# Second pass over grouped count blocks, third pass with one exponent per slot, in a graph kernel on one Trainium2 core

## What is computed

```python
def sage(x, W_l, b_l, W_r):                 # first layer pair, called twice (32 -> 64, relu, 64 -> 32)
    agg = segment_sum(x[src], dst)
    return agg @ W_l.T + b_l + x @ W_r.T
x = layernorm(x + sage(relu(sage(x, ...)), ...))
en, ev = (x @ W2s + b2s)[src], (x @ W2d + b2d)[dst]          # 2 heads x 32
e = sum(leaky_relu(en + ev) * attn, -1)                      # one score for each edge and head
alpha = segment_softmax(e, dst)
msg = softmax(en * r * alpha, axis=-1)                       # over the 32 features of a head
x = layernorm(x + (x + segment_sum(msg, dst).sum(heads)) @ W1 + b1)
```

## Time and profile before

| | us |
|---|---|
| runs, median of 3 (lowest to highest) | 4073.04 (4067.71 to 4081.34) |
| the profiled execution's own time | 4068.59 |
| its span, first to last instruction | 4066.6 |
| first pass and set-up, until the gathers of the second begin | 1091.7 |
| second pass, first gather to the stage after it | 1091.7 to 1801.5 |
| third pass, first gather to the end of the last | 1870.0 to 3898.5 |
| messages of the last slots, output | 3898.5 to 4066.6 |

### The profile page before, as it was taken

One profiled execution on the slowest core, in us unless ns is written; L12 is line 12 of the kernel. 1 busy time (PEld: TensorE's weight loads), 2 busy tenths in 40 slices (PEclk: granted clock), 3 DMA queues, 4 the chain that ended last, 5 costly groups with the idle time before them and its releaser, 6 DMA issues. The chain is left out here.

```text
span 4066.6 us, 79597 instructions
## 1 busy us (share of the span) xinstructions
PE 3054.0 (75%) x26497; PEld 2336.8 (57%) x26497; DVE 2564.1 (63%) x7531; ACT 2697.1 (66%) x7419; POOL 2903.5 (71%) x2913
## 2 busy tenths in 40 slices
PE   4899999999798998885566666766766667666655
PEld 2555555666466666665465555665656666556544
DVE  7987766555422222235357777778777787777776
ACT  4888888778665556641056767777668766677745
POOL 4677777776377777755777777777777777777735
PEclk9999999999899999997657777777667776677767
DMA  2455565555588888853333333333333433343311
GB/s 79 186 207 207 211 234 208 206 207 206 195 310 279 291 289 284 284 173 107 64 86 85 83 81 87 89 86 84 79 82 93 91 83 83 77 92 87 87 31 41
DMA packets 294489, 592.92 MB, mean 146 GB/s; under 512 B 121210, under 2 KB 205364, under 8 KB 286169
## 3 DMA queue, kind: packets, MB, share of 16 engines
q1 hardware_dynamic: 203920, 515.15, 36.0%
q0 software_dynamic: 88192, 72.56, 11.0%
q10 hardware_dynamic: 1969, 0.10, 0.0%
HBM read 384.60 MB, written 202.94 MB: 144 GB/s over the span
## 5 line engine op out<-in xcount | busy, mean ns | idle before, releaser
L897 ACT ACTIVATE scratch<-sum_x_ps_c 128x600 bf16<-128x600 f32 (+7 forms) x1003 | 775.4, 826 | 168.1 <-PE sum_x_ps_c L934 156.5
L1945 POOL DMA_INDIRECT scratch<-fs_scratch,src_idx x728 | 725.3, 996 | 221.9 <-issue 221.9
L834 POOL DMA_INDIRECT gath<-in_x,src_idx x620 | 673.2, 1086 | 277.4 <-issue 182.4
L834 POOL DMA_INDIRECT gath<-y_scratch,src_idx x540 | 524.2, 971 | 171.6 <-issue 163.4
L2073 ACT ACTIVATE scratch<-scratch,bias,weight 128x32 f32<-128x32 f32 x1360 | 484.0, 399 | 101.5 <-DVE bias L2143 101.5
L1987 PEld LDWEIGHTS ps_e<-fdw,scratch 128*128 128x128 f32 x3136 | 500.4, 242 | 24.2
L934 PE MATMUL sum_x_ps_c<-e_tab,scratch 128*128 128x300 bf16 (+7 forms) x2006 | 472.9, 323 | 51.9 <-DVE scratch L1012 32.3
L1009 DVE TENSOR_SCALAR e_tab<-scratch 128x1300 bf16<-128x1300 f16 (+13 forms) x1024 | 455.7, 458 | 61.0 <-PE sum_x_ps_c L934 53.0
L1987 PE MATMUL ps_e<-fdw,scratch 128*128 128x66 f32 x3136 | 482.7, 322 | 0.0
L2154 DVE SCALAR_TENSOR_TENSOR scratch<-ps_e,attn_sb 128x128 f32<-128x128 f32 x784 | 190.2, 285 | 424.3 <-PE ps_e L1987 423.3
L963 PEld LDWEIGHTS sum_x_ps_d<-parts,scratch 128*128 128x128 bf16 x5800 | 337.1, 98 | 158.7 <-ACT scratch L897 68.0
(11 more groups left out here) (341 smaller groups left out, 6362.9 us busy)
## 6 DMA issues: line engine op xcount, KB each, us to landing
count_scratch<-scratch SPq DMA_DIRECT2D x58, 3200.0 KB
scratch<-count_scratch SPq DMA_DIRECT2D x232, 800.0 KB
onehot<-rel_scratch SPq DMA_DIRECT2D x196, 256.0 KB
scratch<-in_edge_attr_2x SPq DMA_DIRECT2D x390, 128.0 KB
fdw<-fd_scratch SPq DMA_DIRECT2D x392, 33.0 KB
scratch<-fs_scratch,src_idx POOLq DMA_INDIRECT x728
gath<-in_x,src_idx POOLq DMA_INDIRECT x652
gath<-y_scratch,src_idx POOLq DMA_INDIRECT x540
```

Source lines behind the costliest of these rows:

```text
L834: pool.indirect_dma_start(out=gath[:, s, t, 0:F], out_offset=None, in_=table_dram, in_offset=bass.IndirectOffsetOnAxis(ap=src_idx[:, g, k: ...
L897: act.activation(to, ps_c[u % pairs][:, :, 0:q].rearrange("p h (d a) -> p h a d", d=d), ACT.Copy).then_inc(kept, 1)
L1945: pool.indirect_dma_start(out=rows_of(m)[:, t, :], out_offset=None, in_=fs_dram, in_offset=bass.IndirectOffsetOnAxis(ap=src_idx[:, g, k:k ...
```

## The change

In the second pass the 58 read blocks are taken in groups of 4 (the last has 2). The roles of the operands are swapped: the 96 feature columns of one high index are the weights, and the counts of 4 blocks (4 x 128 columns) move, so that a group takes 100 matmuls of 512 columns into a 96 x 512 result. It is loaded in 10 pieces of 10 high indices, 4 pieces in flight in four buffers (two of them in memory that the features leave free, so the fourth waits for the cut of the features). After a group ACT copies the result (copy), PE turns it back and adds the three parts with 4 small matmuls (turn), DVE builds 4 placements and copies (spread), PE moves 4 windows, DVE adds them. The steps of the plan are now pieces.

In the third pass, for slots with a step m, DVE subtracts the maxima from the rows and multiplies with the attention weights (two tensor_tensor of 128 x 512 with broadcast operands), ACT runs one exponent of 128 x 512, and DVE sums all of it (L2178 becomes 128 x 512). The copy and the biases go. The one-hots of even slots move from DVE to ACT.

```diff
-QUARTERS = 4
-SHARES = 2 * QUARTERS
+TOGETHER = 4
+HIGHS = 10
+PIECES = ALL_HIGHS // HIGHS
+HELD_PIECES = 4
...
-        self.weight = [66.0 * ALL_HIGHS / SHARES] * (SHARES * self.read) + [0.0]
+        self.groups = [list(range(b, min(b + TOGETHER, self.read))) for b in range(0, self.read, TOGETHER)]
...
+        for r, group in enumerate(self.groups):
+            for i in range(PIECES):
+                self.pieces_at[len(self.weight)] = (r, i)
+                self.weight.append(HIGHS * (P * len(group) / 2.4 + 10.0))
...
-                for i in range(SHARES):
-                    self.products.setdefault(step + i, []).append((r, i, SHARES))
-                self.order.append(r)
-                self.ends(r, step + SHARES)
+            if r < count:
+                for table, later in ((self.copy_at, 0), (self.turn_at, 2), (self.spread_at, 3), (self.windows_at, 4),
+                                     (self.adds_at, 5)):
+                    table[step + PIECES + later] = r
...
-                    return ps_c[2][:, 0, 0:3 * F] if read and j % 2 else ps_d[:, 0:3 * F]
+                    return ps_c[2][:, 1, 0:3 * F] if read else ps_d[:, 0:3 * F]
...
+                def group_product(r):
+                    return (ps_c[2][:, 0, :] if r % 2 else ps_d[:, :])[0:3 * F, 0:len(plan.groups[r]) * P]
...
+                def window_of(i=None):
+                    if i is None:
+                        return ps_s[3 * F:4 * F, 0:WINDOW] if read else ps_s[2 * F:3 * F, 0:WINDOW]
+                    return ps_s[2 * F:3 * F, i * WINDOW:(i + 1) * WINDOW]
...
-                    for b in range(read):
-                        for i in range(QUARTERS):
-                            if b and i == QUARTERS - 1:
-                                sp.wait_ge(multiplied, plan.place[b - 1] + 1)
-                            elif b:
-                                sp.wait_ge(quarter_used, (b - 1) * (QUARTERS - 1) + i + 1)
-                            rows = slice(NK * i // QUARTERS, NK * (i + 1) // QUARTERS)
-                            sp.dma_start(counts[:, 0, rows, :].rearrange("p a q -> p (a q)"),
-                                         count_dram[b, :, rows.start * P:rows.stop * P])\
-                              .then_inc(loaded[i], 16)
+                    for n in range(len(plan.groups) * PIECES if read else 0):
+                        r, i = divmod(n, PIECES)
+                        group, rows = plan.groups[r], slice(i * HIGHS * P, (i + 1) * HIGHS * P)
+                        if n >= HELD_PIECES:
+                            sp.wait_ge(piece_used, n - HELD_PIECES + 1)
+                        elif n == 3:
+                            sp.wait_ge(cut, cuts)
+                        sp.dma_start(piece_of(n).rearrange("p b a q -> p b (a q)"),
+                                     count_dram[group[0]:group[-1] + 1, :, rows].rearrange("b p q -> p b q"))\
+                          .then_inc(loaded[n % HELD_PIECES], 16)
...
+                        if read and step in plan.copy_at:
+                            r = plan.copy_at[step]
+                            act.wait_ge(group_done, r + 1)
+                            if r:
+                                act.wait_ge(group_turned, r)
+                            act.activation(feature_rows[:, 0:len(plan.groups[r]) * P], group_product(r), ACT.Copy)\
+                               .then_inc(group_copied, 1)
...
+                        if read and step in plan.turn_at:
+                            r = plan.turn_at[step]
+                            pe.wait_ge(group_copied, r + 1)
+                            if r:
+                                pe.wait_ge(group_spread, r)
+                            else:
+                                pe.wait_ge(stack_made, 3)
+                            if own_products:
+                                pe.wait_ge(summed_up, own_products)
+                            groups_turned = r + 1
+                            for i, b in enumerate(plan.groups[r]):
+                                m = pe.matmul(group_ps[:, i, :], feature_rows[:, i * P:(i + 1) * P], stack[:, :],
+                                              start=True, stop=True)
+                            m.then_inc(group_turned, 1)
...
+                        if read and step in plan.windows_at:
+                            r = plan.windows_at[step]
+                            pe.wait_ge(group_spread, r + 1)
+                            if r:
+                                pe.wait_ge(group_added, sum(map(len, plan.groups[:r])))
+                            for i, b in enumerate(plan.groups[r]):
+                                columns = head.blocks[b]["columns"]
+                                m = pe.matmul(window_of(i), group_sums[0:columns, i, :], group_places[0:columns, i, :],
+                                              start=True, stop=True)
+                            m.then_inc(group_windowed, 1)
+                        if read and step in plan.pieces_at:
+                            r, i = plan.pieces_at[step]
+                            n = r * PIECES + i
+                            pe.wait_ge(loaded[n % HELD_PIECES], n // HELD_PIECES * 16 + 16)
+                            if n == 0:
+                                pe.wait_ge(cut, cuts)
+                            if i == 0 and r >= 2:
+                                pe.wait_ge(group_copied, r - 1)
+                            for a in range(HIGHS):
+                                m = pe.matmul(group_product(r).rearrange("p (b q) -> p b q", q=P),
+                                              parts[:, i * HIGHS + a, :], piece_of(n)[:, :, a, :],
+                                              start=(i == 0 and a == 0), stop=(i == PIECES - 1 and a == HIGHS - 1))
+                            m.then_inc(piece_used, 1)
+                        if read and step - 1 in plan.pieces_at and plan.pieces_at[step - 1][1] == PIECES - 1:
+                            r = plan.pieces_at[step - 1][0]
+                            pe.wait_ge(piece_used, (r + 1) * PIECES)
+                            pe.sem_inc(group_done, 1)
...
-                            if b < read and i % 2 == 0:
-                                pe.wait_ge(loaded[i // 2], b * 16 + 16)
+                                if groups_turned:
+                                    pe.wait_ge(group_spread, groups_turned)
...
+                        if read and step in plan.spread_at:
+                            r = plan.spread_at[step]
+                            dve.wait_ge(group_turned, r + 1)
+                            if r:
+                                dve.wait_ge(group_windowed, r)
+                            for i, b in enumerate(plan.groups[r]):
+                                dve.tensor_scalar(group_places[:, i, :], iota[:, :], head_rel[:, b:b + 1], None,
+                                                  ALU.is_equal)
+                            blocks = len(plan.groups[r])
+                            dve.tensor_copy(group_sums[:, 0:blocks, :], group_ps[:, 0:blocks, :])\
+                               .then_inc(group_spread, 1)
+                        if read and step in plan.adds_at:
...
+                            for i, b in enumerate(group):
+                                if groups_added:
+                                    dve.wait_ge(group_added, groups_added)
+                                to = table_a[2 * F:3 * F, bass.ds(firsts[i], WINDOW)]
+                                dve.tensor_tensor(to, to, window_of(i), ALU.add).then_inc(group_added, 1)
+                                groups_added += 1
...
-                return on_vector(n, 0) or (0 < n <= TAIL and n % 2 == 0)
+                return on_vector(n, 0)
...
-                            act.activation(rows_of(n)[:, :, 0:HID], rows_of(n)[:, :, 0:HID], ACT.Exp).then_inc(exp_done, 1)
                         else:
-                            act.wait_ge(bias_ready, n + 1)
-                        for i in range(ST * H if m is not None else 0):
-                            rows = rows_of(n)[:, i // H, i % H * F:(i % H + 1) * F]
-                            e = act.activation(rows, rows, ACT.Exp, bias=bias[:, q, i:i + 1],
-                                               scale=weight[:, q, i:i + 1],
-                                               accum_out=total[:, q, i:i + 1] if i < K * H else None)
-                        if m is not None:
-                            e.then_inc(exp_done, 1)
+                            act.wait_ge(weighted, n + 1)
+                        act.activation(rows_of(n)[:, :, 0:HID], rows_of(n)[:, :, 0:HID], ACT.Exp).then_inc(exp_done, 1)
...
-                        dve.tensor_copy(weight[:, q, :],
-                                        attention_of(n))
+                        heads = rows_of(n)[:, :, 0:HID].rearrange("p t (h f) -> p t h f", h=H)
                         dve.wait_ge(top_ready, n + 1)
```

(9 more changed lines are left out.)

84 lines of the change are left out of this document (62 added, 22 removed).

## The result

The changed kernel takes 4092.16 us (median of 4 runs, 4090.30 to 4096.73), the kernel before 4070.38 beside it (4 runs, 4067.61 to 4081.34): a ratio of 1.0056, interval 1.0041 to 1.0072. It is slower by 0.56%, 22 us. The predicted time was 4083 with a range of 4058 to 4112; the likeliest case, within 0.3%, did not come.

A forecast was written before the change was run, and what follows sets the result against it. POOL's gather stream was taken to bound both passes. Second-pass end +1, DVE's lateness +2.5 and lengthened gathers +7 gave +10.5 on the profiled 4068.6, 4079; on the median 4083 us, range 4058 to 4112.

The forecast's parts named there:

- three ways in which the time could change: Lengthened gathers, what is left after the last gather, or an engine that becomes slower than POOL's stream.
- Rival A: Third pass: new operations fall between beginnings of gathers and L2170's 23 us go; -20, 4053 us; chance 0.18.
- Rival B: Third pass: the 1.4 us pair outlasts the 1.25 between gather beginnings, holding one nearly every slot; +49, 4122; chance 0.15.
- net +7 of the lengthened gathers: Third pass: new DVE operations add 30 us of gather lengthening, L2170 gives back 23; bounds -23 and +45.
- credit for L2170: DVE's even-slot one-hots leave: 52 us by d squared / 2.5 for each operation, with factor 0.44 gives back 23.
- pair of new operations: Third pass, DVE's subtraction and multiplication: 68 us of lengthened gathers by the formula, 30 by the factor 0.44.
- Second pass: +1: After the last gather, one more PE and DVE link, about 2 us, less some give-back; bounds -8 and +10.
- give-back: End of the second pass: clustered tail tiles return some of the about 2 us of added links.
- dearer bound: Second pass, PE: a 512-column matmul costs 213 to 236 ns, the sum 309 to 342 us; 309 taken.
- hidden reserve: Second pass: PE's 85 us idle hide the 19 us more that the swapped products cost it.
- DVE's lateness at the end: Third pass, last four steps: DVE's added work reaches the end; +2.5 us, bounds 0 and +6.
- C: PE becomes the bound of the second pass, only with a lower granted clock; some +20, 4093 us; chance 0.07.

The follow-up runs named there:

- third-pass half alone: Only the third-pass diff, on the kernel before, second pass untouched; measured singly 4090.8 against 4077.5 us, 1.0035.
- kernel with PSUM operands: Changed kernel with the third pass's maxima, attention weights and reciprocal sums in PSUM; 4083.7 against 4079.3 us for the kernel before, 1.0014.

## Why the prediction was right and wrong

**What bounds the kernel: right.** POOL's stream sets both passes after the change as before, with only "issue" ahead of its gathers. The mean gather of the third pass is 1569.9 / 1564 = 1.004 us, near the 1000 ns that the forecast named and between its marks for rivals A (975) and B (1020). DVE rose by 123 us in the stretch, 110 were forecast. The three ways in which the time could change were the right three, and the largest is lengthened gathers.

**The term that was mis-sized is the net +7 of the lengthened gathers; it was +17.7**, and +18.2 with the third-pass half alone. Inside it the credit for L2170 is the larger error. The prediction took -23 from its formula and its factor, and the trace agrees that this stands under that line (22.8). Taken out alone it gave 5.4 us (1552.2 to 1546.8). The pair of new operations was put at +30; the rest of the third-pass half, which is the pair, the longer sum and the two small operations that go, costs 1570.4 - 1546.8 = 23.6: the smaller error, on the other side. So the whole miss, and more, is the credit. These are differences of single traces; the medians say the same, 8.6 us for the credit where 23 were taken. The prediction had the reason in its own sentence, that one hold protects the next operation, and used it for a factor on what is added but not for what is taken away. In the traces the r multiplication, which follows the scaling of the slot, went from 9.6 to 22.2 us when L2170 was gone. An operation's share of lengthening is what it holds beside the others, not what its removal gives back.

**Rival B's sentence was half right.** A beginning does fall into the pair about once in a slot: 116 of the 177 multiplications and 66 of the subtractions had one. But the chain keeps its distance from the gathers, so the multiplication is met 0.35 us after its start and costs some 0.21 us each time, the subtraction 0.07. Rival A relied on the same constant distance and hoped that it fell outside; it falls inside.

**Second pass: +1 was taken, +2.6 measured between the passes**, within its bounds of -8 and +10. The added links are seen at its end, timelines of POOL, PE and DVE:

```profile
1782.58 0.95 POOL L872 DMA_INDIRECT gath<-y_scratch,src_idx  x1 [0.30 <-issue]
```

```profile
1799.03 1.72 PE L1071 MATMUL sum_y_ps_s<-onehot,gath 128*32 128x128 f32 x14
1800.68 0.63 PE L1006 MATMUL sum_y_ps_c<-scratch 96*128 96x32 f32 x4
...
1802.41 0.62 PE L1016 MATMUL sum_y_ps_s<-scratch 126*32 126x128 f32 x4 [0.77 <-DVE scratch L1139]
```

```profile
1803.18 0.72 DVE L1156 TENSOR_TENSOR table_a<-table_a,sum_y_ps_s 32x128 f32 x2 [0.50 <-PE sum_y_ps_s L1016]
```

The turn (L1006) follows the own block's product and 14 tail tiles, then spread, window and add: the last add ends 20.4 us after the last gather, against 17.95 before. The give-back that the prediction subtracted did not come.

PE's price came out at its dearer bound. The products of the groups, second pass:

```profile
L1028 PE MATMUL sum_y_ps_d<-scratch,parts 128*96 128x512 bf16 x420 | 107.3, 406 | 15.6 <-ACT parts L903 13.7 <-DMA scratch<-count_scratch 1.9
...
L1028 PE MATMUL sum_y_ps_c<-scratch,parts 128*96 128x512 bf16 x280 | 65.9, 382 | 0.8 <-DMA scratch<-count_scratch 0.8
...
L1028 PE MATMUL sum_y_ps_c<-rest,parts 128*96 128x512 bf16 x210 | 52.6, 400 | 1.0 <-DMA rest<-count_scratch 1.0
L1028 PE MATMUL sum_y_ps_c<-nodes,parts 128*96 128x512 bf16 x210 | 51.2, 393 | 0.5 <-DMA nodes<-count_scratch 0.5
L1028 PE MATMUL sum_y_ps_d<-rest,parts 128*96 128x512 bf16 x140 | 33.0, 382 | 0.0
L1028 PE MATMUL sum_y_ps_d<-nodes,parts 128*96 128x512 bf16 x140 | 32.9, 382 | 0.0
```

A piece of ten in the timeline:

```profile
1400.96 2.36 PE L1028 MATMUL sum_y_ps_d<-rest,parts 128*96 128x512 bf16 x10
```

That is 236 ns for a matmul, the dearer bound, and not the 2.1 us for ten that the forecast expected to see. The busy times add up to 342.9 us for 1400, 245 ns each with the interleaving, over the dearer bound (342 with the 100 of 256 columns) rather than at the 309 taken. PE's busy time in the pass rose by 11 us (604 to 615), and its waiting for gathers fell from 66.7 to 51.0 us: the hidden reserve paid, as said. The waits for loads in these rows are 4.2 us, against 0.6 + 3.4 before, at the same DMA share of 0.84: the finer runs of 2560 bytes cost PE nothing to be seen, though the prediction held them dearer for each byte. The Trainium skill's price in TensorE: Matmul & The Clock Gate, section Back-to-back issue gap (about 131 ns for 512 columns) is not what the trace shows: 236 ns, at a granted clock of 0.97.

**DVE's lateness at the end: +2.5 was taken, it can't be seen.** Behind the last gather lie 168.3 us after against 168.1 before; the kernels of the experiments scatter from 168.6 to 170.7.

**ACT's saving was worth nothing in time, as said; its size was told wrongly**: 589 us in the third pass, not 900. The 900 had left out the one-hots that come (427.4 / 1400 us for each small pass, eight and a long one of 1.15: 3.6 us in every second slot, some 320 us).

**The inference of the Trainium skill** (SBUF — State Buffer, section Who interferes with whom), that tensor_tensor doesn't hold descriptor generation, is contradicted by the traces here for these indirect gathers: 1.99 us beside L2170 before, 1.156 us in the mean under L2258 after, against 0.944. The same section's rule that two SBUF inputs contend with a GpSimd instruction that reads SBUF fits these gathers, and the 250 of 946 ns under operations with one input in PSUM agree with it.

**The chances.** The forecast had an own range of -4 to +22 with 0.13 of its 0.60 beyond +12; the result lies at that end, +21.8 by the medians and +24.2 by the two profiles. That the range to +39 holds it owes as much to the room left for rivals B and C, which did not come, as to the sum. With the credit at -5 instead of -23 the sum would have been 1 + 2.5 + 25 = 28, and "slower" the likeliest.

## What to carry to other kernels

When one engine's stream sets the pace and another engine's operations hold it up, price an operation that goes by taking it out, not by what stands under its line: its neighbours can take over most of it (here 17 of 23 us), until only few holders are left. The size of one hold is simple: what is left of the operation shortly after the held work begins, so the distance between the two streams decides it. Work moved off an engine with cover is worth nothing by itself; here the room that it made on ACT paid in the kernel in which DVE's holding one-hot moved there and the holding operands went to PSUM. And the cover is part of the result: the same second-pass edit cost some 3 us where POOL set the pace, and took out 168 in executions in which POOL waited for PE.

## What was not expected of the hardware

A tensor_tensor with one operand in PSUM does not hold an indirect gather (946 ns mean of 250), with both in SBUF it does (up to 1.99 us), and the gather then ends 0.81 to 0.83 us after the operation (all 228 of the changed kernel); a tensor_scalar of 128x1024 from f16 to f32 in SBUF does too (1.40 us at 2134.90), a tensor_reduce of 128x512 does not (66 gathers in the kernel with PSUM operands, mean 946 ns, longest 962). The operand's place costs DVE nothing (0.69 us either way).
